# Local attention layers with the next layer's first tile computed inside the last feed-forward groups

## The chip, the cores and the metric

One Trainium2 chip, one of its cores. The metric is the time of the whole program on the device in microseconds, as the median of several runs. All data are float32, except where a table of masks and an identity are bfloat16.

## What is computed

The input is one sequence of 2048 tokens of width 128. A softmax attention block and its norm come first, then a stack of six local attention layers, then a linear attention block, then the same stack of six again, then a residual sum. The change is in the stack alone, which is run twice (its tensors have the prefixes `f_` and `g_`). Reduced to what matters, a stack is:

```python
for layer in range(6):
    h = shift_tokens(x)                       # the upper 64 features are those of the token before
    q, k, v = split(h @ Wqkv[layer], 3)       # 16 heads of 64
    q, k = l2norm(q) * q_scale, l2norm(k) * k_scale
    q, k = rotary(q, xpos_scale), rotary(k, 1 / xpos_scale)
    # token i sees keys i-32 .. i
    x = softmax(8 * q @ k.T + mask) @ v @ Wo[layer] + x
    h = layernorm(shift_tokens(x)) * g + b
    a, gate = split(h @ W1[layer] + b1, 2)    # hidden width 341
    x = (a * gelu(gate)) @ W2[layer] + b2 + x
```

## The kernel before, in words

`local_stack` (from L625) writes one instruction list by hand for each engine, as functions with the same names: `tile`, `group` and, for all, `layer`. Semaphores join them. `upto(s, L, n)` (L645) is the count that semaphore `s` has once item `n` of layer `L` is done, so an engine waits for exactly the item it needs. A loop `Fori(0, DEPTH)` runs over the six layers.

**Attention.** The 2048 tokens are 16 tiles of 128. A tile has four chunks `c`, and a step is `n = 4 t + c`, 64 steps (`STEPS`) in a layer. Chunk by chunk the projections of q half 0, k half 0, q half 1 and k half 1 are made (L1168), and in chunks 0 and 2 the values (L1185). The work of a step is spread over the following chunks, and the test `real(t, c, lag)` says whether step `n - lag` exists:

- lag 0: PE projects; ScalarE squares (L984); VectorE sums the squares (L1073); POOL raises to the power -1/2 (L928).
- lag 1: VectorE scales (L1067) and multiplies with two rope tables (L1094, L1096); POOL adds the two (L933).
- lag 2: PE transposes (L1237); ScalarE copies to `qT` or `kT` (L1013 to L1017).
- lag 4: PE makes masked scores of four heads (L1195, L1202); VectorE the maximum (L1078); ScalarE four exponentials (L1002).
- lag 5 to 7: VectorE normalises (L1084, L1087); PE transposes (L1173); ScalarE copies (L988); PE multiplies with the values (L1221); ScalarE copies to `aT` (L1024).
- In chunk 3 PE multiplies tile t-2 with `Wo` (L1231); in chunk 0 VectorE adds the residual of tile t-3 (L1063), and SP stores it to `xa` in DRAM (L843).

The values of a tile are copied to `vt` (L994), two buffers. Three transfers on SP's queue (L827 to L829) move them, with the last 32 rows of the tile before, to the windows `vw` that the value product reads. A copy to `vt` waits for the transfers of tile t-1, since these read the same buffer. For tile 1 this is the wait

```python
act.wait_ge(ld_vw[1 - q], upto(ld_vw[1 - q], L, (t - 1) >> 1, 48))
```

The tiles 0 to 2 and 13 to 15 are written out, the others are a `Fori` over pairs. After tile 15, the chunks of "tiles" 16 to 18 hold what is left of the lags.

**Feed-forward.** It has 8 groups of 256 tokens (`NF`). Stage `m` of `group` holds three groups at once: VectorE's statistics of group m+1 (L1103, L1107) and POOL's inverse deviation (L937, L939), VectorE's normalise of group m (L1119), PE's transposes (L1253) and ScalarE's Identity with gain and bias (L1033); for group m-1 PE's hidden products in three pairs (L1260, L1261), ScalarE's Gelu (L1038) and VectorE's product (L1137), giving `ag`; for group m-2 PE's output product (L1268), with POOL's bias sum (L951); and for group m-3 VectorE's output sum (L1127, `fy`) and SP's store to `xf` (L866). The hidden products have two sets of three PSUM banks.

**Between them.** Stages 0 and 1 come after the chunks of tiles 16 and 17, and stages 2 to 10 after those of tile 18. In stages 0 and 1 POOL also multiplies the rope tables with the next layer's scales (`fold_rope`, L914, L917). SP's queue is written out by hand as well: at tile 16 the next layer's `Wqkv` (L800) and the first shifted rows for the feed-forward (L852, L853), in stage 2 `Wo` (L807), in stage 6 the next layer's first two x tiles (L792, L793), in stage 9 the feed-forward weights, which are 13 transfers (L810 to L818), and in stage 10 the last store of `fy`. At the head of the layer loop PE transposes x (L1157), ScalarE copies it (L976), and the projections start.

Of the kernel before, what the change touches and what calls it, by code (L numbers as in the profile page):

```python
# [624 lines left out]
def local_stack(nc, tag, w, consts, xf, xa):  # L625
# [6 lines left out]
    with ExitStack() as ctx:  # L632
# [85 lines left out]
        STEPS = 4 * NT  # L718
        ld_ident, ld_rope, ld_mask, zeroed, act_const = (sem("ld_ident"), sem("ld_rope"), sem("ld_mask"), sem("zeroed"),
# [20 lines left out]
        dv_kzero, pl_rope = sem("dv_kzero", 1, 1), sem("pl_rope", 6)  # L740
# [13 lines left out]
        def layer(eng, body, group, L, last):  # L754


            for t in range(3):
                body(L, t, t % 2)
            with eng.Fori(0, (NT - 6) // 2) as i:
                for q in range(2):  # L760
                    body(L, 2 * i + (3 + q), (3 + q) % 2)
            for t in range(NT - 3, NT):
                body(L, t, t % 2)

            for t in range(NT, NT + 3):
                if t < last:
                    body(L, t, t % 2)
                if t < NT + 2:
                    group(L, t - NT, t % 2)
            groups(eng, group, L)  # L770

        def groups(eng, body, L):


            for m in range(2, NF + 3):
                body(L, m, m % 2)
# [19 lines left out]
        def _(sp):  # L796
# [23 lines left out]
            def tile(L, t, q):  # L820
# [12 lines left out]
                if known and t == NT:  # L833
                    sp.wait_ge(pe_qkv, upto(pe_qkv, L, STEPS - 1)).then_inc(own["sp"], 1)
                    sp.wait_ge(pl_rope, upto(pl_rope, L, 5)).then_inc(own["sp"], 1)
                    load_scales((L + 1) % DEPTH)
                    load_wqkv((L + 1) % DEPTH)
                    load_shifted(L, 0, 0)
                    load_shifted(L, 1, 1)
# [4 lines left out]
                if not known or 0 <= t - 2 < NT:  # L844
                    sp.wait_ge(st_a, upto(st_a, L, t - 4, 16)).then_inc(own["sp"], 1)
                    sp.dma_start(xr[:, q, :], rows(xf, (t - 2) * P + 1, P)).then_inc(ld_r[q], 16)

# [7 lines left out]
            def group(L, m, q):  # L855
                known = isinstance(m, int)
                if not known or m + 2 < NF:
                    load_shifted(L, m + 2, q)
                if not known or 0 <= m - 1 < NF:
# [3 lines left out]
                if not known or m >= 3:  # L863
# [5 lines left out]
                if known and m == 2:  # L869
                    sp.wait_ge(pe_Wo, upto(pe_Wo, L, NT - 1)).then_inc(own["sp"], 1)  # L870
                    load_wo((L + 1) % DEPTH)
# [18 lines left out]
            sp.wait_ge(zeroed, 5)  # L890
            with sp.Fori(0, DEPTH) as L:
                layer(sp, tile, group, L, NT + 3)

            for p in range(2):
                sp.wait_ge(ld_x[p], upto(ld_x[p], DEPTH, 0, 32))
# [7 lines left out]
        def _(pool):  # L903
# [5 lines left out]
            def fold_rope(n, kind):  # L909

                pool.wait_ge(ld_scales, upto(ld_scales, n, 0, 32))
                whole = qk_scales[:, kind, :].unsqueeze(1).broadcast_to([P, NT, DH])
                halves = qk_scales[:, kind, :].rearrange("p (a b) -> p a b", a=2)[:, ::-1, :]
                pool.tensor_tensor(rope[:, 2 * kind, :, :], rope0[:, 2 * kind, :, :], whole, ALU.mult).then_inc(pl_rope, 1)  # L914
                for a in range(2):
                    sl = slice(a * 32, a * 32 + 32)
                    pool.tensor_tensor(rope[:, 2 * kind + 1, :, sl], rope0[:, 2 * kind + 1, :, sl],  # L917
                                       halves[:, a, :].unsqueeze(1).broadcast_to([P, NT, 32]),
                                       ALU.mult).then_inc(pl_rope, 1)

            def tile(L, t, q):
                for c in range(4):
                    n, b = 4 * t + c, c % 2
                    if real(t, c, 0):

                        pool.wait_ge(dv_ssq, upto(dv_ssq, L, n)).then_inc(own["pool"], 1)
                        pool.wait_ge(dv_qh, upto(dv_qh, L, n - 2))
                        pool.tensor_tensor(rn[:, b, :], ss[:, b, :], minus_half[:], ALU.pow).then_inc(pl_rn, 1)  # L928
                    if real(t, c, 1):

                        pool.wait_ge(dv_t2, upto(dv_t2, L, n - 1))
                        pool.wait_ge(pe_qkT, upto(pe_qkT, L, n - 3))
                        pool.tensor_tensor(qr[:, 1 - b, :], t1[:, 1 - b, :], t2[:, 1 - b, :], ALU.add).then_inc(pl_qr, 1)  # L933
# [7 lines left out]
            def group(L, m, q):  # L941
                known = isinstance(m, int)
                if known and m == 0:
                    inverse_std(L, 0, 0)
                if not known or m + 1 < NF:
                    inverse_std(L, m + 1, 1 - q)
                if not known or 0 <= m - 2 < NF:
# [5 lines left out]
                if known and m < 2:  # L953
                    pool.wait_ge(dv_t2, upto(dv_t2, L, STEPS - 1))
                    fold_rope(L + 1, m)
# [3 lines left out]
            fold_rope(0, 0)  # L959
            fold_rope(0, 1)  # L960
            with pool.Fori(0, DEPTH) as L:
                layer(pool, tile, group, L, NT + 1)

        @block.scalar
        def _(act):
# [12 lines left out]
            def tile(L, t, q):  # L978
                for c in range(4):
                    n, b = 4 * t + c, c % 2  # L980
                    if real(t, c, 0):
                        act.wait_ge(pe_qkv, upto(pe_qkv, L, n))
                        act.wait_ge(dv_ssq, upto(dv_ssq, L, n - 2))
                        act.activation(sq[:, b, :], ps_qk[b][:], ACT.Square).then_inc(act_sq, 1)  # L984
                    if real(t, c, 6):
                        act.wait_ge(pe_pT, upto(pe_pT, L, n - 6))
                        act.wait_ge(pe_o, upto(pe_o, L, n - 8))
                        act.copy(pT[0:KEYS, b, :, :], ps_pT[0:KEYS, :].rearrange("p (u q) -> p u q", u=4)).then_inc(act_pT, 1)  # L988
                    if c % 2 == 0 and real(t, c, 0):
                        half = c // 2  # L990
                        act.wait_ge(pe_v, upto(pe_v, L, 2 * t + half))

                        act.wait_ge(ld_vw[1 - q], upto(ld_vw[1 - q], L, (t - 1) >> 1, 48))
                        act.copy(vt[:, q, 512 * half:512 * half + 512], ps_v[:]).then_inc(act_v, 1)  # L994
                    if c == 1 and real(t + 1, 0, 0):
# [702 lines left out]
```

## Time and profile before

| | |
|---|---|
| median of 3 runs | 5309.06 us (5306.06 to 5313.56) |
| the profiled execution | 5306.88 us |
| its span in the trace | 5304.9 us |
| stack `f`, first square to last output sum | 992 to 3025 us |
| stack `g`, first square to last output sum | 3244 to 5277 us |
| mean granted TensorE clock | 0.956 |

Two microseconds of the profiled execution lie outside the span. Each stack is some 2034 us of it, or 340 us a layer. In the rows that follow, PE is TensorE's matmul stream and PEld its weight loads, DVE is VectorE, ACT ScalarE, POOL GpSimd, and SPq the issue of transfers by SyncE. In rows of the timeline the numbers are start and duration in us; what stands in square brackets is the idle time before and what ended it ("issue" is nothing that the profile shows).

### The profile page before, as it was taken

The numbers are of one execution on the slowest core, as the hardware profiler recorded it, in microseconds if no ns is written. First come the engines' busy times: TensorE is split into PE (matmuls) and PEld (weight loads), VectorE is DVE, ScalarE is ACT, GpSimd is POOL, SyncE is SP. The second block draws the span as 40 slices with busy tenths as digits, with TensorE's granted clock in tenths as the row PEclk, the third lists the DMA queues.
The fourth block names the chain that finished last, engine by engine and source line by source line (L and its number), as shares of the span: only waits on it lengthen the run. The fifth ranks groups of instructions, "written<-read, shape, count | busy, mean of one in ns | idle before, by whom it ended". The sixth has DMA issues, their size and how long they took to land. (4 is left out here: it accounts for less than half of the span.)

```text
span 5304.9 us, 148219 instructions
## 1 busy us (share of the span) xinstructions
PE 4683.4 (88%) x45702; PEld 2936.7 (55%) x45796; DVE 4006.0 (76%) x8097; ACT 3640.1 (69%) x11776; POOL 2657.8 (50%) x2108
## 2 busy tenths in 40 slices
PE   5999999698998998989989767989989989899896
PEld 1333332366565665656666544665656656566665
DVE  7888886587786877868778546878868778687785
ACT  1777777586785876858768514867858768587684
POOL 3000000465665656656656404656656566566564
PEclk6999999899999999999999877999999999999998
DMA  0000000222222222222222302222222222222223
GB/s 13 1 2 1 2 1 1 85 58 73 57 59 77 59 71 59 59 77 59 65 66 59 85 5 85 60 75 56 57 78 60 71 61 56 77 60 69 66 54 93
DMA packets 332305, 288.20 MB, mean 54 GB/s; under 512 B 149102, under 2 KB 290964, under 8 KB 329748
## 3 DMA queue, kind: packets, MB, share of 16 engines
q1 hardware_dynamic: 331028, 281.93, 20.6%
q8 instruction: 254, 4.16, 0.3%
q14 instruction: 255, 2.09, 0.1%
q10 hardware_dynamic: 768, 0.02, 0.0%
HBM read 100.42 MB, written 30.41 MB: 25 GB/s over the span
## 5 line engine op out<-in xcount | busy, mean ns | idle before, releaser
L928 POOL TENSOR_TENSOR f_rn<-f_ss,f_minus_half 128x8 f32<-128x8 f32 x384 | 636.9, 1658 | 302.0 <-DVE f_ss L1073 297.1
L928 POOL TENSOR_TENSOR g_rn<-g_ss,g_minus_half 128x8 f32<-128x8 f32 x384 | 636.8, 1658 | 301.2 <-DVE g_ss L1073 296.3
L425 DVE TENSOR_REDUCE a_maxima<-a_max 128x1 f32<-128x512 f32 x1024 | 651.8, 687 | 147.4 <-PE a_max L539 110.4
L1002 ACT ACTIVATE f_ex<-f_bank,f_nmx 128x96 f32<-128x96 f32 x1536 | 502.9, 339 | 226.3 <-DVE f_nmx L1078 226.3
L1002 ACT ACTIVATE g_ex<-g_bank,g_nmx 128x96 f32<-128x96 f32 x1536 | 502.9, 339 | 226.2 <-DVE g_nmx L1078 226.2
L349 ACT ACTIVATE a_pex<-a_scores 128x512 f32<-128x512 f32 x1024 | 531.6, 606 | 159.3 <-PE a_scores L548 158.5
L933 POOL TENSOR_TENSOR g_qr<-g_t 128x512 f32<-128x512 f32 x384 | 488.4, 1272 | 269.6 <-DVE g_t L1096 269.6
L933 POOL TENSOR_TENSOR f_qr<-f_t 128x512 f32<-128x512 f32 x384 | 488.4, 1272 | 268.7 <-DVE f_t L1096 268.7
L1168 PE MATMUL g_bank<-g_wqkv,g_xT 128*128 128x512 f32 x768 | 407.9, 614 | 29.9 <-ACT g_xT L976 24.1
L1168 PE MATMUL f_bank<-f_wqkv,f_xT 128*128 128x512 f32 x768 | 407.0, 612 | 29.9 <-ACT f_xT L976 24.5
L1073 DVE TENSOR_REDUCE f_ss<-f_sq 128x8 f32<-128x512 f32 x384 | 263.5, 686 | 209.7 <-ACT f_sq L984 195.4
L1073 DVE TENSOR_REDUCE g_ss<-g_sq 128x8 f32<-128x512 f32 x384 | 263.5, 686 | 209.0 <-ACT g_sq L984 195.6
L539 PE MATMUL a_max<-a_stackT 128*128 128x512 bf16 x963 | 345.8, 396 | 22.1 <-DVE a_maxima L425 14.0
L280 POOL COPY a_v_head<-a_v_all 128x128 f32 (+1 forms) x16 | 4.6, 290 | 694.2 <-PE a_sums L557 694.2
L548 PE MATMUL a_scores<-a_stackT 128*128 128x512 bf16 x991 | 308.6, 382 | 27.3 <-ACT a_pex L349 20.2
L1002 ACT ACTIVATION_READ_ACCUMULATOR f_ex<-f_bank,f_nmx 128x1 f32 x1536 | 311.4, 203 | 0.0
L1002 ACT ACTIVATION_READ_ACCUMULATOR g_ex<-g_bank,g_nmx 128x1 f32 x1536 | 311.3, 203 | 0.0
L1237 PE MATMUL f_bank<-f_ident,f_qr 128*128 128x128 f32 x1536 | 248.3, 284 | 47.9 <-POOL f_qr L933 47.3
L1237 PE MATMUL g_bank<-g_ident,g_qr 128*128 128x128 f32 x1536 | 248.7, 285 | 47.5 <-POOL g_qr L933 46.3
L1173 PEld LDWEIGHTS f_bank<-f_ident,f_pn 128*96 128x96 f32 x1536 | 173.3, 126 | 206.7 <-DVE f_pn L1087 123.2
L1173 PEld LDWEIGHTS g_bank<-g_ident,g_pn 128*96 128x96 f32 x1536 | 172.9, 126 | 207.0 <-DVE g_pn L1087 122.9
L1067 DVE SCALAR_TENSOR_TENSOR f_qh<-f_rn,f_bank 128x512 f32<-128x512 f32 x384 | 261.5, 681 | 28.8 <-POOL f_rn L928 28.8
(238 smaller groups left out, 12000.6 us busy)
## 6 DMA issues: line engine op xcount, KB each, us to landing
f_vw<-f_vt SPq DMA_DIRECT2D x96, 384.0 KB, 4.2
g_vw<-g_vt SPq DMA_DIRECT2D x96, 384.0 KB, 4.3
f_vw<-f_vt SPq DMA_DIRECT2D x96, 256.0 KB, 3.6
g_vw<-g_vt SPq DMA_DIRECT2D x96, 256.0 KB, 3.6
f_vw<-f_vt SPq DMA_DIRECT2D x96, 128.0 KB, 2.3
g_vw<-g_vt SPq DMA_DIRECT2D x96, 128.0 KB, 2.3
f_wqkv<-in_f_Wqkv_dram SPq DMA_DIRECT2D x7, 1536.0 KB, 9.5
g_wqkv<-in_f_Wqkv_dram SPq DMA_DIRECT2D x7, 1536.0 KB, 9.3
```

The lines of the kernel that those rows point to most:

```text
L349: act.activation(pex[:, kt % 2, i % NG, :], ps_s[i % 3][:], ACT.Exp).then_inc(act_ex, 1)
L425: dve.tensor_reduce(maxima[:, m // 4, m % 4:m % 4 + 1], ps_max[m % 3][:], AX.X, ALU.max).then_inc(dv_max, 1)
L539: pe.matmul(ps_max[m % 3][:], stackT[:, slot, 0, P * (m // 4):P * (m // 4) + P], stackT[:, slot, 1, GQ * (m % 4):GQ * (m % 4) + GQ], start ...
L548: pe.matmul(ps_s[i % 3][:], stackT[:, slot, 1, P * kt:P * kt + P], stackT[:, slot, 0, GQ * g:GQ * g + GQ], start=True, stop=True).then_inc ...
L928: pool.tensor_tensor(rn[:, b, :], ss[:, b, :], minus_half[:], ALU.pow).then_inc(pl_rn, 1)
L933: pool.tensor_tensor(qr[:, 1 - b, :], t1[:, 1 - b, :], t2[:, 1 - b, :], ALU.add).then_inc(pl_qr, 1)
L1002: last = act.activation(ex[:, b, u, :], ps_s[:, h, KEYS * jj:KEYS * jj + KEYS], ACT.Exp, bias=nmx[:, b, u:u + 1], accum_out=sm[:, b, u:u + 1])
L1067: dve.scalar_tensor_tensor(out=heads(qh[:, 1 - b, :]), in0=rn[:, 1 - b, :].unsqueeze(2).broadcast_to([P, 8, DH]), scalar=1e12, in1=heads(p ...
L1073: dve.tensor_reduce(ss[:, b, :], heads(sq[:, b, :]), AX.X, ALU.add).then_inc(dv_ssq, 1)
L1168: pe.matmul(ps_qk[b][:], xT[:, q, :], wqkv[:, at:at + 512], start=True, stop=True).then_inc(pe_qkv, 1)
L1173: last = pe.transpose(ps_pT[0:KEYS, P * u:P * u + P], pn[:, b, u, :], ident[:])
L1237: last = pe.transpose(ps_qkT[:, P * j:P * j + P], qr[:, b, P * j:P * j + P], ident[:])
```

## The change

The loop over layers is rotated. `tile` becomes `chunk`, one call for one chunk, and `group` becomes `stage`. The four chunks of tile 0 of the next layer run inside stages 6 to 9 of this layer; the first layer's are run by `head` ahead of the loop. In the last layer of the stack they are computed as well, and nothing reads them. The left-over chunks 64 to 72 are dealt out over stages -2 to 2.

- The statistics start two stages ahead and the normalise one stage ahead. On PE the first hidden pair comes before the transposes, and on ScalarE the first Gelu before the Identity; on VectorE the output sum comes first and the three products are spread between the others.
- PSUM banks are dealt out anew (`ps_f`, `ps_h`, `freed`). From group 2 on the hidden products have one set of banks, 6, 7 and 4.
- The rope tables are folded in four slices of four tiles, in stages 1 to 4, both kinds in each.
- On SP's queue the first shifted rows are loaded at tile 15 and `Wqkv` last in tile 16; the next x tiles and `Wo` in stage 4; and the feed-forward weights in stage 10, after the last store of `fy`. The v windows of tile 0 are issued by tile 1's chunk 0, after the jump to the loop's head.

Its core (the bodies that are only moved one level out are left out):

```diff
-        ps_h = [[banks[0], banks[7], banks[3]], [banks[4], banks[6], banks[2]]]
-        ps_fT = banks[1]
-        ps_f = banks[5]
+        ps_f = [banks[0 if m < 3 else 5] for m in range(NF)]
+        ps_h = [[banks[i] for i in ((1, 3, 6), (7, 1, 3))[m]] if m < 2 else [banks[6], banks[7], banks[4]] for m in range(NF)]
+        freed = [-6, -6, -6, -6, 0, 1, 2, 3, -6]
...
+            seam = [(-2, 1), (-1, 1), (0, 2), (1, 2), (2, 3)]
+            n = STEPS
+            for m, chunks in seam:
+                stage(L, m)
+                for k in range(n, n + chunks):
+                    chunk(L, k // 4, k // 4 % 2, k % 4)
+                n += chunks
+            for m in range(3, 6):
+                stage(L, m)
+            for m in range(6, 10):
+                stage(L, m)
+                chunk(L + 1, 0, 0, m - 6)
+            stage(L, NF + 2)
...
         # SP, stage
-                if known and m == NF - 2:
+                if m == 4:
                     for p in range(2):
                         sp.wait_ge(pe_xT, upto(pe_xT, L, NT - 2 + p)).then_inc(own["sp"], 1)
                         load_xs(sp, L + 1, p, p)
-                if known and m == NF + 1:
+                    sp.wait_ge(pe_Wo, upto(pe_Wo, L, NT - 1)).then_inc(own["sp"], 1)
+                    load_wo((L + 1) % DEPTH)
+                if m == NF + 2:
                     sp.wait_ge(pe_out, upto(pe_out, L, NF - 1)).then_inc(own["sp"], 1)
                     sp.wait_ge(pl_b2, upto(pl_b2, L, NF - 1)).then_inc(own["sp"], 1)
                     load_wf((L + 1) % DEPTH)
...
         # POOL, stage
+                if 0 <= m - 1 < NR:
                     pool.wait_ge(dv_t2, upto(dv_t2, L, STEPS - 1))
-                    fold_rope(L + 1, m)
+                    fold_rope(L + 1, NT // NR * (m - 1), NT // NR, 1)
+                if m + 2 < NF:
+                    inverse_std(L, m + 2, q)
...
         # ACT, stage
+                if 0 <= m - 1 < NF:
+                    gelu(L, m - 1, 0)
+                if 0 <= m < NF:
...
+                    act.activation(xnT[:, m % 2, :], ps_f[m][:, 0:FQ], ACT.Identity, bias=ln_b[:], scale=ln_g[:]).then_inc(act_fT, 1)
+                if 0 <= m - 1 < NF:
+                    gelu(L, m - 1, 1)
+                    gelu(L, m - 1, 2)
...
         # DVE, stage: output sum (m - 3), product 0 (m - 1), normalise (m + 1), product 1 (m - 1),
         # statistics (m + 2), product 2 (m - 1); at m == 2 also the memset of kT's first columns
...
         # PE, stage
+                if 0 <= m - 1 < NF:
+                    pe.wait_ge(act_fT, upto(act_fT, L, m - 1))
+                    hidden(L, m - 1, 0)
+                if 0 <= m < NF:
...
+                        last = pe.transpose(ps_f[m][:, P * s:P * s + P], xn[:, m % 2, s, :], ident[:])
...
+                if 0 <= m - 1 < NF:
+                    hidden(L, m - 1, 1)
+                    if m == 1:
+                        pe.wait_ge(act_exp, upto(act_exp, L, STEPS - 1))
+                    hidden(L, m - 1, 2)
+                if 0 <= m - 2 < NF:
+                    # the output product of group m - 2 waits for its products, for sum m - 3
+                    # and for the Identity of group m
...
         # PE, chunk
+                if known and n == 0:
+                    pe.wait_ge(dv_y, upto(dv_y, L - 1, NT - 1)).then_inc(own["pe"], 1)
+                    transpose_x(L, 0, 0)
+                    pe.wait_ge(ld_wqkv, upto(ld_wqkv, L, 0, 16))
```

## Rows read from the trace of the kernel before

**Rows 1.** The page, busy time and share of the span by engine.
```profile
PE 4683.4 (88%) x45702; PEld 2936.7 (55%) x45796; DVE 4006.0 (76%) x8097; ACT 3640.1 (69%) x11776; POOL 2657.8 (50%) x2108
```
**Rows 2.** Stretches: length, busy PE, PEld, DVE, ACT, POOL, granted clock; steady attention, drain.
```profile
1564.00:1598.00 34.00, 33.37 (x395) 22.57 (x393) 29.40 (x59) 28.62 (x106) 23.37 (x16) 1.00 0.22 56
1598.00:1617.00 19.00, 14.94 (x230) 11.63 (x228) 11.43 (x29) 13.79 (x58) 6.39 (x6) 1.00 0.48 144
```
**Rows 3.** Timeline, layer 1: last square, last scores, output of tile 14, first statistics.
```profile
1598.33 0.64 ACT L984 ACTIVATE f_sq<-f_bank 128x512 f32<-128x512 f32 x1
...
1612.88 0.56 PE L1202 MATMUL f_bank<-f_kT,f_qT 64*64 64x96 f32 x16
...
1613.99 2.05 PE L1231 MATMUL f_bank<-f_wo,f_aT 128*128 128x128 f32 x16
...
1614.66 0.48 DVE L1103 BATCH_NORM_STATS2 f_st<-f_fxs 128x6 f32<-128x128 f32 x2
...
1615.29 0.25 DVE L1107 BATCH_NORM_AGGREGATE f_mv<-f_st 128x2 f32<-128x6 f32 x2 [0.15 <-DVE f_st L1103]
...
1616.79 0.60 DVE L1119 TENSOR_SCALAR f_xn<-f_fxs,f_mv,f_rstd 128x128 f32<-128x128 f32 x2 [1.25 <-POOL f_rstd L939]
```
**Rows 4.** Timeline, layer 1's feed-forward: slow and full pairs, transposes of groups 3 and 6.
```profile
1631.06 1.02 PE L1261 MATMUL f_bank<-f_xnT,f_w 128*128 128x256 f32 x2
...
1636.65 0.44 PE L1253 MATMUL f_bank<-f_ident,f_xn 128*128 128x128 f32 x2 [0.25 <-DVE f_xn L1119]
...
1637.36 0.59 PE L1261 MATMUL f_bank<-f_xnT,f_w 128*128 128x256 f32 x2
...
1650.51 0.44 PE L1253 MATMUL f_bank<-f_ident,f_xn 128*128 128x128 f32 x2 [0.25 <-DVE f_xn L1119]
```
**Rows 5.** Timeline, end of layer 1 and start of layer 2.
```profile
1665.83 0.42 DVE L1127 TENSOR_TENSOR f_fy<-f_bank,f_fx 128x256 f32<-128x256 f32 x1 [1.85 <-DMA xf<-f_fy]
1666.02 0.37 SPq L810 DMA_DIRECT2D f_w<-in_f_W_dram  x1
...
1668.48 0.35 PE L1157 MATMUL f_bank<-f_ident,f_xs 128*128 128x128 f32 x1 [2.77 <-issue]
...
1674.52 0.40 SPq L866 DMA_DIRECT2D xf<-f_fy  x1
...
1686.53 0.59 ACT L994 COPY f_vt<-f_bank 128x512 f32<-128x512 f32 x1 [0.33 <-PE f_bank L1185]
...
1689.75 0.63 ACT L984 ACTIVATE f_sq<-f_bank 128x512 f32<-128x512 f32 x1
```
**Rows 6.** Timeline, the seam before: layer 0's last square, layer 1's value copy and square.
```profile
1256.99 0.64 ACT L984 ACTIVATE f_sq<-f_bank 128x512 f32<-128x512 f32 x1
...
1348.04 0.59 ACT L994 COPY f_vt<-f_bank 128x512 f32<-128x512 f32 x1 [1.17 <-PE f_bank L1185]
...
1350.99 0.63 ACT L984 ACTIVATE f_sq<-f_bank 128x512 f32<-128x512 f32 x1
```
**Rows 7.** Busy time in stretches as in rows 2, after the jump between layers 0 and 1.
```profile
1327.30:1334.10 6.80, 4.58 (x6) 2.03 (x7) 0.69 (x1) 2.36 (x4) 0.44 (x1) 0.50 0.22 41
```
**Rows 8.** Timeline, POOL: the bias sum over 256 columns, and a rope fold over 1024.
```profile
1638.91 0.72 POOL L951 TENSOR_TENSOR f_fx<-f_fx,f_b 128x256 f32<-128x256 f32 x1
...
1619.68 2.35 POOL L914 TENSOR_TENSOR f_rope<-f_rope,f_qk_scales 128x1024 f32<-128x1024 f32 x1
```
**Rows 9.** The page's transfers: the largest of the three v windows, median to landing.
```profile
f_vw<-f_vt SPq DMA_DIRECT2D x96, 384.0 KB, 4.2
```
**Rows 10.** Timeline, end of stack f: first of the 13 weight loads, last store.
```profile
3025.24 0.37 SPq L810 DMA_DIRECT2D f_w<-in_f_W_dram  x1
...
3031.80 0.40 SPq L866 DMA_DIRECT2D xf<-f_fy  x1
```
**Rows 11.** Instructions of lines L976 and L1038: the table loads among them.
```profile
L976 ACT ACT_TABLE_LOAD  x12: 1283/1283/1283, 988.5 to 4939.4; - x12
L1038 ACT ACT_TABLE_LOAD  x12: 1283/1283/1283, 1284.2 to 5236.7; - x12
```

More of the change, by code:

```diff
@@ L890, in _ @@
             sp.wait_ge(zeroed, 5)
+            head(chunk)
             with sp.Fori(0, DEPTH) as L:
-                layer(sp, tile, group, L, NT + 3)
+                layer(sp, chunk, stage, L)
             for p in range(2):
-                sp.wait_ge(ld_x[p], upto(ld_x[p], DEPTH, 0, 32))
+                sp.wait_ge(ld_x[p], upto(ld_x[p], DEPTH, 1 - p, 32))
             sp.wait_ge(ld_wqkv, 16 * (DEPTH + 1))
@@ L907, in _, with fold_rope @@
             pool.memset(kT[:], 0.0).then_inc(zeroed, 1)
-            def fold_rope(n, kind):
+            def fold_rope(n, first, count, each):
                 pool.wait_ge(ld_scales, upto(ld_scales, n, 0, 32))
[L912 to L933, printed above, removed]
+                ts = slice(first, first + count)
@@ L939, in inverse_std, with stage @@
                 pool.tensor_tensor(rstd[:, q, :], var[:, q, :], minus_half[:, 0:FT], ALU.pow).then_inc(pl_rstd, 1)
[L941 to L947, printed above, removed]
+            def stage(L, m):
+                q = m % 2
+                if 0 <= m - 2 < NF:
                     pool.wait_ge(ld_wf, upto(ld_wf, L, 0, 13 * 16))
@@ L1044, in _ @@
             put_mask()
+            head(chunk)
             with act.Fori(0, DEPTH) as L:
-                put_xT(L, 0, 0)
-                act.wait_ge(dv_kzero, upto(dv_kzero, L, -1))
-                layer(act, tile, group, L, NT + 2)
+                layer(act, chunk, stage, L)
         @block.vector
@@ L1140, in _ @@
+                if m + 2 < NF:
+                    row_stats(L, m + 2, m % 2)
+                if 0 <= m - 1 < NF:
+                    product(L, m - 1, 2)
+                if m == 2:
+                    dve.wait_ge(pe_s, upto(pe_s, L, STEPS - 1))
+                    dve.memset(kT[:, :, P:P + WINDOW], 0.0).then_inc(dv_kzero, 1)
             for buf in (vt, vw, pT):
                 dve.memset(buf[:], 0.0).then_inc(zeroed, 1)
+            head(chunk)
             with dve.Fori(0, DEPTH) as L:
[L1143 removed]
@@ L1144, in _ @@
-                layer(dve, tile, group, L, NT + 3)
-                dve.wait_ge(pe_s, upto(pe_s, L, STEPS - 1))
-                dve.memset(kT[:, :, P:P + WINDOW], 0.0).then_inc(dv_kzero, 1)
+                dve.wait_ge(pl_rope, upto(pl_rope, L, 6 * NR - 1)).then_inc(own["dve"], 1)
+                layer(dve, chunk, stage, L)
         @block.tensor
@@ L1275, in _ @@
             pe.wait_ge(ld_ident, 16)
+            head(chunk)
             with pe.Fori(0, DEPTH) as L:
-                transpose_x(L, 0, 0)
-                pe.wait_ge(ld_wqkv, upto(ld_wqkv, L, 0, 16))
                 pe.wait_ge(ld_wo, upto(ld_wo, L, 0, 16)).then_inc(own["pe"], 1)
-                layer(pe, tile, group, L, NT + 2)
+                layer(pe, chunk, stage, L)
 def linear_attention(nc, tag, x_in, w, consts, x_out, xf):
```

488 lines of the change are left out of this document (250 added, 238 removed).

## The prediction

> **What bounds the kernel now.** I read the page first: TensorE is busy 88% of the span and VectorE 76% [rows 1], so on average nothing has much to give. That average hides the place of this change. Both local stacks are six layers long, and a layer is a long stretch of attention followed by a feed-forward. The stage table shows the steady attention with PE busy 33.37 of 34.00 us, and the first 19 us of the drain with 14.94 [rows 2]. The change touches only this end, the feed-forward and the next start. So I measure every event from one mark, the start of the layer's last square of a projection on ScalarE, at 1598.33 [rows 3].
>
> From that mark, in this layer: the last scores are computed at +14.6 [rows 3]; group 3 of the feed-forward is transposed at +38.3, group 6 at +52.2 [rows 4]; the last output sum ends at +67.9; PE then idles 2.77 us on "issue", at the jump back to the loop's head; the second 128 tokens' first value copy (f_vt, L994) starts at +88.2, the next square (of step 5) at +91.4 [rows 5]. The seam before took 91.1 and 94.0 [rows 6]: after the jump the granted clock was 0.50 for 6.8 us [rows 7], the lower of the two levels, and in that seam again later. I take the means of the two, +89.6 and +92.7. These are the marks to beat. The stretch is a chain of hand-offs (projection, square, sum, power on POOL, scaling, rope, transposes), not a full engine.
>
> **The change, part by part.** Ten seams between layers have the whole change; the last layer of each stack has all its costs and no next layer.
>
> Drain and groups 0 to 2. Statistics and normalising (0.48 + 0.15 + 0.25 and 0.60) go between the last chunks. The first statistics fit in VectorE's idle time; the next ones and the first normalise come before the maximum of step 61 and push it by 0.75. The Identity copy (0.57) on ScalarE falls in the same chain, so the last scores start at +15.2 and not +14.6, and the last exponentials end at +17.8 [rows 3]. PE does the output sum of tile 14 (2.05) and then group 0's first hidden pair, ended at +19.4. Table load (1.28), three Gelus (0.47 each) and the Identity bring ScalarE to +22.5; VectorE's three products, a normalise, statistics and the delayed probabilities end at +24.8. PE's last probability transpose and value product go to +26.0, group 1's hidden pairs and a transpose (2.6 + 0.3) to +28.9, group 0's output (1.42) to +30.3, the last value product, its copy and the output of tile 15 to +33.5, one hidden pair (0.86), and group 3 is transposed at +34.4 where it was +38.3. In the old order the granted clock fell here once; a pair at the low level takes 1.02 to 1.06 where it takes 0.59 [rows 4]. I add 1.0 for the same fall (bounds 0 and 1.4): +35.4, so **2.9 won**.
>
> Groups 3 to 5. The old period is 4.62 ((52.2 - 38.3) / 3): the transposes wait 0.25 for a normalise that stands behind the last product [rows 4]. In the new order a hidden pair covers that wait. PE's own work is 0.27 + 3 x 0.86 + 1.42 = 4.28. One set of hidden banks where there were two costs nothing: a bank is free as soon as its product is made, 1.6 us after its pair starts, and is wanted 4.28 later. The rope fold is the same work in four slices; POOL needs about 0.7 for 256 columns [rows 8], so a slice is about 3.2, and with a bias sum (0.73) and the inverse deviation (about 1.0) a stage is 5.0. It begins a stage early and has slack from the seam. Statistics of group 5 wait for SP, held until tile 15's row store: 0.3. Three stages are 13.1: group 6 at +48.5, **3.7 won** so far.
>
> Groups 6, 7 and the end, with four chunks of the next layer. The old stretch from here to the last sum is 15.7. New, along PE: rest of stage 6 3.4; x transpose, copy, first projection and values 2.5; stage 7 4.6, of which 0.3 waits for the output sum, which is behind a square sum on VectorE; chunk 1 1.15; stage 8 4.4, 0.4 of it such a wait; chunk 2 2.2; stage 9 3.2, 1.8 of it such a wait (behind two rope products); then projection 3, square, square sum, two rope products and the last output sum, 1.02 + 0.65 + 0.7 + 1.25 + 0.42 = 4.0. Sum 25.4: the last sum ends at +73.9, **6.0 later** than before, but with four steps done that used to take 13.7 us from first to fifth square.
>
> The wait that replaces the start-up. From here the engines could go on at once: the fifth square would come about 2 us later, near +76, and the value copy at +77.3. But the copy overwrites a buffer that the three v-window copies read, and ScalarE waits for these transfers. SP issues them after the jump, and in the new order the 13 loads of the next feed-forward weights stand in front. Before, they started when the last output product ended, 0.2 before the last sum was done, and lay beside the start-up [rows 5]. Now SP waits for the last output sum, stores it, waits as before for PE and POOL, issues 13 loads, and only then the v windows. Chain: 0.2 to SP, 0.5 for the store, 8.5 for the loads to the next issue [rows 5], 0.3 for the loop's end, 1.2 until the third window's issue, 4.2 to its landing [rows 9]: 14.9. Bounds: 6.6 for the loads as at a stack's end [rows 10] gives 13.0; a landing a microsecond later behind the weights gives 15.9. The copy starts at +88.8, against +89.6. Queued behind it on ScalarE are all the exponentials, so PE stands idle some 11 us. On release the exponentials need not wait for the maximum, which has long been there, so the next square is 2.4 behind the copy, not 3.1: 0.7 won. The idle time surely costs clock: an idle of 2.77 was followed by 6.8 us at 0.50 [rows 5, 7]. During the restart this costs between 0 and 3.4; I take 0.9, since hand-offs fill most of it.
>
> One seam: -0.8 - 0.7 + 0.9 = -0.6 us; ten: **-6**.
>
> Ends of the stacks. The last layer computes four useless chunks, so its last sum is 6.0 later. Before, the last store was issued 6.6 after the first weight load [rows 10], so 6.3 after the sum, whose end is 0.2 behind that load's issue [rows 5]; it landed about 2 later. Now the store goes first, but the block ends with the weight loads, some 9.2 after the sum, 0.8 more. Twice 6.8: **+13.6**. The start of each stack has the same steps in the same order: nothing.
>
> Sum +7.6 on the profiled execution's own 5306.9 is 5314.5. That execution lies 2.2 below the median 5309.1, so 5316.7, rounded down to **5316 us**. About 0.2%, 10.6 us, is what a measurement of this kernel can tell from no change; the forecast lies within it, near its edge.
>
> **The rivals.**
> *A, the wait does not bite*: the start-up is simply hidden. For it: the engines would be at the copy by +77.3. A seam then gains 12.3, so 5309 - 123 + 14 = 5200. Against it: SP issues in order, and the loads' time is in the trace. Chance 0.06.
> *B, the merged stretch runs better*: no fall of the clock in the drain (1.0) or during the release (0.9), no late statistics (0.3), and 6.6 us of loads (1.9). Each seam gains 4.1 more: 5275. For it: bounds of mine, each seen once. Against: all must hold. 0.17.
> *C, slower: VectorE's order sets the merged stages.* The output sum stands behind the chunk's square sum and rope products, and PE's transposes or output stand behind that sum. My waits of 0.3, 0.4 and 1.8 are differences of long sums. If each of the four pairs takes 1 us more, the last sum, SP's loads and the copy all shift by 4: 10 x 4 + 2 x 4 is 48 at most, less where the low clock hides in a wait; 5355. It decides from 0.6 us a seam upwards, where nothing is won any more. Chance 0.22.
> *D, table loads.* There are two per layer, 1.28 each, one at the first Gelu and one at the loop's head [rows 11]; squares and exponentials share one set, and no row shows a square under Gelu's. If it needs the other set, a seam has four more loads, two at squares and two at Gelus, about 5 us, all ahead of the last sum: 5316 + 12 x 4.5 = 5370. Chance 0.05. The Trainium skill (ScalarE: Activation LUTs, Table sets: the hidden batching unit) speaks against the interleaving: activations are to be batched by set. The same section says that cheap functions such as copy and identity stand in every set, without naming the square there, and its section What ACT_TABLE_LOAD costs puts a switch at 2.66 us with the drain; by that figure the four would cost about 10.6 us a seam. The trace has 1.28 for the load itself and an Identity and Gelus side by side with no further load.
>
> **How the numbers follow.** The forecast as worked has 0.50, with its own range 5296 to 5336; of this 0.05 is faster by over 0.2%, 0.29 within, 0.16 slower. A and B are faster, C and D slower. Faster 0.05 + 0.06 + 0.17 = 0.28, within 0.29, slower 0.16 + 0.22 + 0.05 = 0.43. The range 5276 to 5356 takes in B and C and leaves out A, D and the tails.
>
> **What would show it.** In the changed kernel: group 3 transposed about +35 and a period of 4.3 for groups 3 to 5; the last output sum near +74; ScalarE idle some 11 us before the value copy of every layer's tile 1 but the first, ended by the f_vw transfer; the 13 weight loads between the last store and the v windows on SP's queue; low clock in that gap; two table loads a layer. The prediction is wrong if that copy waits for nothing (A), if the last sum comes before +71 (B) or after +76 (C), or if squares have table loads before them (D).

## The result, and the profile after

The changed kernel takes 5428.5 us (median of 4 runs, 5423.2 to 5430.0), the kernel before on the same chip 5307.6: ratio 1.023, 95% interval 1.0217 to 1.0242. That is 121 us slower. The forecast was 5316 with a range to 5356, so it was **wrong** in the size. "Slower" had the largest of its three chances, 0.43, but the point that it gave lay within 0.2% of the kernel before. The profiled execution has a span of 5420.7 us against 5304.9.

The page, busy time by engine. These lines answer to [rows 1]:
```profile
PE 4725.8 (87%) x45840; PEld 2958.5 (55%) x45840; DVE 3989.7 (74%) x8123; ACT 3639.7 (67%) x11798; POOL 2706.7 (50%) x2338
```
No engine does much more work. PE is busy for 42 us more, with 138 more instructions and a lower mean clock (0.941, before 0.956). The rest of the 116 us is idle time of PE, and the question is what it waits for.

I measured both kernels as the prediction does, from the start of a layer's last square (here 1605.40), and took the mean over the ten seams. The column "forecast" repeats the prediction's marks. Differences in the text are taken before rounding.

| start at, us after the mark | before | forecast | after | after, stack f | after, stack g |
|---|---|---|---|---|---|
| last scores | 14.5 | 15.2 | 19.6 | 19.2 | 19.9 |
| group 3 transposed | 38.3 | 35.4 | 40.1 | 39.9 | 40.4 |
| group 6 transposed | 52.2 | 48.5 | 55.2 | 54.8 | 55.5 |
| end of the last output sum | 68.0 | 73.9 | 80.5 | 80.0 | 81.1 |
| first weight load issued | 67.7 | about 74.6 | 81.6 | 80.9 | 82.3 |
| first v window issued | 81.5 | - | 91.9 | 88.9 | 94.8 |
| value copy of tile 1 | 89.6 | 88.8 | 97.5 | 94.6 | 100.4 |
| square of step 5 | 92.7 | 91.2 | 99.7 | 96.8 | 102.6 |

Three losses are to be read from it. In both stacks the last scores are over 4 us later than forecast. Groups 3 to 5 take 15.0 us instead of 13.1. And stack g loses another 4.5 us between the first weight load and the first v window (12.5 us against 8.0 in f). The stretch with the four chunks of the next layer, from group 6 to the last output sum, takes 25.4 us, as forecast.

Timeline, the drain of layer 1: SyncE's queue first, then VectorE and ScalarE, then PE. What stands in brackets is the idle time before the row and what ended it:
```profile
1612.99 0.33 SPq L809 DMA_DIRECT2D f_wqkv<-in_f_Wqkv_dram  x1
1614.92 0.39 SPq L864 DMA_DIRECT2D f_fxs<-xa  x1
1615.36 0.75 SPq L865 DMA_DIRECT2D f_fxs<-xa  x1
...
1616.73 0.60 DVE L1154 TENSOR_SCALAR f_xn<-f_fxs,f_mv,f_rstd 128x128 f32<-128x128 f32 x2
...
1621.24 0.48 DVE L1121 BATCH_NORM_STATS2 f_st<-f_fxs 128x6 f32<-128x128 f32 x2 [3.90 <-DMA f_fxs<-xa]
...
1622.09 0.56 DVE L1096 TENSOR_REDUCE f_nmx<-f_bank 128x4 f32<-128x384 f32 x1
...
1622.68 0.34 ACT L1015 ACTIVATE f_ex<-f_bank,f_nmx 128x96 f32<-128x96 f32 x1 [3.32 <-DVE f_nmx L1096]
...
1624.72 0.92 PE L1231 MATMUL f_bank<-f_kT,f_qT 64*64 64x96 f32 x16
1626.62 2.75 PE L1260 MATMUL f_bank<-f_wo,f_aT 128*128 128x128 f32 x16
```
The rows of group 2 (f_fxs) are issued 1.9 us behind the next layer's Wqkv. VectorE's statistics of group 2 want them at 1617.34 and get them at 1621.24. The maximum of step 62 is behind these statistics in VectorE's order, ScalarE's exponentials wait for it, and the last scores (1624.72, +19.3) wait for those. The page's transfers show the size of what is ahead:
```profile
f_wqkv<-in_f_Wqkv_dram SPq DMA_DIRECT2D x7, 1536.0 KB, 7.9
f_fxs<-xa SPq DMA_DIRECT2D x96, 64.0 KB, 3.1
```
1612.99 + 7.9 is 1620.9, just before the statistics start. In the kernel before, this load was issued at 1600.14, 1.8 us behind the mark and not 7.6, and nobody waited for the rows behind it: the statistics came behind the attention and, at 1614.66, had no wait [rows 3].

The same drain as a stretch (columns as in rows 2); it answers to the second line there:
```profile
1605.40:1624.60 19.20, 13.14 (x182) 9.86 (x174) 13.02 (x36) 11.85 (x49) 9.45 (x13) 0.82 0.48 144
```
The granted clock is 0.82 where it was 1.00: the scores take 0.92 and the output product 2.75, where they took 0.56 and 2.05 [rows 3]. All twelve drains of this kernel have 6.8 or 10.2 us at the lower level, starting 12 to 15 us behind the mark. Before, there was one fall of 3.4 us, near +32.

Groups 3 to 5, SyncE's queue in stage 4 and VectorE in stage 5:
```profile
1651.03 0.40 SPq L801 DMA_DIRECT2D f_xs<-xf  x1
...
1653.13 0.39 SPq L816 DMA_DIRECT2D f_wo<-in_f_Wo_dram  x1
1653.91 0.37 SPq L864 DMA_DIRECT2D f_fxs<-xa  x1
1654.41 0.38 SPq L865 DMA_DIRECT2D f_fxs<-xa  x1
...
1657.99 0.48 DVE L1121 BATCH_NORM_STATS2 f_st<-f_fxs 128x6 f32<-128x128 f32 x2 [1.47 <-DMA f_fxs<-xa]
```
Four loads of x and one of Wo (2.9 us of SyncE) stand ahead of the rows of group 7, which are wanted at 1656.52.

The end of the layer, where the forecast stall is. Last output sum; SyncE's first and last weight loads and first v window; ScalarE:
```profile
1684.90 0.41 DVE L1142 TENSOR_TENSOR f_fy<-f_bank,f_fx 128x256 f32<-128x256 f32 x1
...
1686.20 1.39 SPq L819 DMA_DIRECT2D f_w<-in_f_W_dram  x1
...
1693.28 0.38 SPq L827 DMA_DIRECT2D f_b<-in_f_b_dram  x1
1694.33 0.56 SPq L838 DMA_DIRECT2D f_vw<-f_vt  x1
...
1686.07 1.28 ACT L997 ACT_TABLE_LOAD   x1 [2.21 <-issue]
1687.45 0.60 ACT L997 ACTIVATE f_sq<-f_bank 128x512 f32<-128x512 f32 x1
1699.81 0.58 ACT L1007 COPY f_vt<-f_bank 128x512 f32<-128x512 f32 x1 [11.76 <-DMA f_vw<-f_vt]
```
This is the wait that the prediction named, at its length ("some 11 us"): 14.5 us from the end of the sum to the copy, 14.9 forecast. In stack g the same wait is 15.4 to 16.8 us.

Groups of instructions by line. Before the bar the busy time and the mean ns, behind it the idle time before the group and what ended it. These are the two waits over all layers:
```profile
L1007 ACT COPY g_vt<-g_bank 128x512 f32<-128x512 f32 x194 | 116.2, 599 | 98.9 <-DMA g_vw<-g_vt 80.1 <-PE g_bank L1214 17.7
L1007 ACT COPY f_vt<-f_bank 128x512 f32<-128x512 f32 x194 | 116.2, 599 | 75.1 <-DMA f_vw<-f_vt 57.1 <-PE f_bank L1214 17.1
L1121 DVE BATCH_NORM_STATS2 g_st<-g_fxs 128x6 f32<-128x128 f32 x96 | 23.0, 281 | 42.9 <-DMA g_fxs<-xa 42.9
L1121 DVE BATCH_NORM_STATS2 f_st<-f_fxs 128x6 f32<-128x128 f32 x96 | 23.0, 281 | 35.7 <-DMA f_fxs<-xa 35.7
```

### The profile page after: what moved, and what is told of

It is laid out like the page before. It is cut to its first block and busy times, and to the rows that moved or that the text cites. A ratio compares the mean times of both kernels' runs of the same rounds, so it can differ in the third digit from the quotient of the medians.

```text
span 5420.7 us, 148975 instructions
## 1 busy us (share of the span) xinstructions
PE 4725.8 (87%) x45840; PEld 2958.5 (55%) x45840; DVE 3989.7 (74%) x8123; ACT 3639.7 (67%) x11798; POOL 2706.7 (50%) x2338
## 5 line engine op out<-in xcount | busy, mean ns | idle before, releaser
L539 PE MATMUL a_max<-a_stackT 128*128 128x512 bf16 x1024 | 369.5, 398 | 12.5 <-issue 6.8
L997 ACT ACTIVATE f_sq<-f_bank 128x512 f32<-128x512 f32 x388 | 241.9, 623 | 60.5 <-PE f_bank L1197 58.2
L997 ACT ACTIVATE g_sq<-g_bank 128x512 f32<-128x512 f32 x388 | 241.9, 623 | 60.1 <-PE g_bank L1197 57.7
L1250 PE MATMUL g_bank<-g_pT,g_vw 128*64 128x64 f32 x6144 | 268.0, 231 | 7.9
```

The lines of the kernel that those rows point to most:

```text
L539: pe.matmul(ps_max[m % 3][:], stackT[:, slot, 0, P * (m // 4):P * (m // 4) + P], stackT[:, slot, 1, GQ * (m % 4):GQ * (m % 4) + GQ], start ...
L1250: last = pe.matmul(ps_o[r, at:at + BLK], vw[:, p, blk, P * j + DH * h:P * j + DH * h + DH], pT[:, 1 - b, 2 * h + jj, BLK * blk:BLK * blk + ...
```

## The experiments

All nine runs that follow are of the changed kernel with the edit named. Two theories went in: **W**, the v windows come late, and **D**, rows for VectorE's statistics come late and hold the attention's last steps. Against them: the merged stages' order (the prediction's rival C), the clock, and the loop's jump. Chips and hours shift both kernels a little, so I compare each run by its distance to the kernel before, measured beside it (the changed kernel: +121). Where an expectation says "the fifth square", it means the square of step 5; only the one "4.3 us behind the last fy" in run 5 is tile 1's first square.

**1. Windows first.** In SyncE's program:
```
 stage 9:        + three copies vw <- vt of tile 0
 chunk of t=1:   - three copies vw <- vt of tile 0
```


> Edit: the three copies that make tile 0's V windows are issued in stage 9, right after the last chunk of tile 0, so ahead of the last fy store, of the 13 weight loads and of the loop's jump, instead of behind all three. Theory W (the windows are late, and ScalarE's second value copy of tile 1 waits for them): the wait of 11.8 us in front of that copy goes, the next limit is the first square of tile 1, which stands 2.7 us behind the last fy. The fifth square behind the last square of the layer before then starts at about +87 instead of +96.7 in stack f and +102.4 in stack g: -10 us in each of five seams of f, -15 in each of g, 5428 - 125 = about 5300 us. Rival J (the jump to the loop's head, 2.9 us on PE, 2.2 on ScalarE and 5.2 on SyncE in stack g, is what is waited for; windows are only the last of it): SyncE is still late in g, PE and ScalarE wait as long for other things, g gains no more than f, 5428 - 70 to 90 = 5340 to 5360. Rival C (the merged stages' order costs everywhere): under 30 us gained.

Measured: 5326.9 us, ratio 1.004 (1.0025 to 1.0054), +23. So 98 of the 121 are gone, less than the 125 expected and far more than rival C allowed. At the square of step 5, stack g gains 10.9 us a seam and f 5.3; rival J allowed g no more than f. The copy of tile 1's values starts 5.9 us behind the last sum (87.8 and 81.9), not 17.0. In the seam of layer 1:
```profile
1683.12 1.28 ACT L1002 ACT_TABLE_LOAD   x1 [3.75 <-issue]
1685.06 0.60 ACT L1002 ACTIVATE f_sq<-f_bank 128x512 f32<-128x512 f32 x1 [0.65 <-PE f_bank L1202]
1686.85 0.59 ACT L1012 COPY f_vt<-f_bank 128x512 f32<-128x512 f32 x1 [1.19 <-PE f_bank L1219]
...
1682.95 2.07 PE L1202 MATMUL f_bank<-f_wqkv,f_xT 128*128 128x512 f32 x2 [4.59 <-issue]
```
The stall is gone, and the jump is next: PE idles 4.59 us there (2.87 with the stall behind it) and ScalarE 3.75 (2.21). In six of the ten seams the clock falls a second time near +30, and the mean distance from group 1's transpose to group 3's grows from 15.3 to 16.9 us. These two are some 1.6 us a seam each. That is of the size of the missing 27, and no closer than that: the profiled execution is 12 us slower than the median.

**2. Wqkv in pieces.**
```
 chunk of t=NT:  - load_wqkv(next layer)            (1.5 MB)
 stages 0 to 5:  + load_wqkv(next layer, piece m)   (256 KB, behind the shifted rows of group m+2)
```


> Edit: the next layer's 1.5 MB of Wqkv is loaded in six pieces of 256 KB, one behind each of the loads of the shifted rows of groups 2 to 7, instead of in one transfer ahead of the rows of group 2. Theory D (VectorE's statistics of group 2 wait 3.9 us for rows that lie behind the 7.9 us of the large load, and the maximum of step 62 stands behind them): that wait shrinks to under 1 us, the layer's last scores come at +15.5 to +16.5 instead of +19.6, group 3's first transpose at +36.5 instead of +40.1, and ten seams of 3.5 us give about 5393 us. Rival K (TensorE's lower clock in the drain, or VectorE's longer order of work, sets it): last scores stay within 1 us of +19.6, time within 10 us of 5428. Rival P (the pieces take the place of the one load and each delays the rows of its stage): last scores earlier by 3.5 us but group 6 as late as before at +55.2, no gain in sum.

Measured: 5364.9 us, 1.0111 (1.0094 to 1.0128), +61. Last scores at +16.8 instead of +19.6, group 3 at +37.2, group 6 at +52.4: theory D holds and most of the gain is carried on, so rivals K and P fall as the main cause. In stack f 1.8 of 2.9 us are left at the square of step 5, where the clock falls near +53 in three of its five seams. In layer 1 the wait is down from 3.90 us to:
```profile
1617.64 0.49 DVE L1123 BATCH_NORM_STATS2 f_st<-f_fxs 128x6 f32<-128x128 f32 x2 [1.08 <-DMA f_fxs<-xa]
```
In stack g it is 0.2 us or less. The low clock in the drains shrinks to 3.4 or 6.8 us, but it does not go away with the wait: five of stack g's six drains still have a fall. The 60 won are more than the 35 expected, because stack g's 4.5 us between weight loads and windows are gone too (7.8 us in f, 8.1 in g). Nothing in the edit touches that place. Run 9 asks why.

**3. x and Wo one stage later**, behind the rows of group 7.
```
 - if m == 4:  load_xs(next layer, tiles 0 and 1), load_wo(next layer)
 + if m == 5:  the same
```


> Edit: the loads of the next layer's first two x tiles and of Wo are issued in stage 5 behind the shifted rows of group 7 instead of in stage 4 ahead of them. Theory Q (the five issues in stage 4 hold SyncE's queue, so the rows of group 7 come late and the statistics of group 7 wait 1.5 us): stage 5 takes about 4.4 instead of 5.9 us, group 6's first transpose comes at +53.7 instead of +55.2, ten seams give 15 us: about 5413. Rival (stage 5 is long for another reason, such as the order of the Gelus and the products): no change, 5428.

Measured: 5402.1 us, 1.0181 (1.0164 to 1.0198), +98. Groups 3 to 5 take 13.0 us, where the forecast had 13.1 and the changed kernel 15.0: theory Q holds. Group 6 comes at +54.2, not +53.7, since a second fall of the clock near +30, as in run 1, puts group 3 at +41.2. Of the 23 us won, 7 lie in the linear attention block, ahead of stack g's first square, which this edit should not touch; run 9 finds the same 7 us there.

**4. Weights behind the windows**, both in tile 1's first chunk, behind the jump.
```
 stage 10:       - load_wf(next layer)
 chunk of t=1:   three copies vw <- vt of tile 0
                 + wait for the last layer's last fy, load_wf(this layer)
```


> Edit: the 13 loads of the feed-forward weights are issued in tile 1's first chunk, behind the copies of tile 0's V windows, instead of ahead of them; the copies stay behind the last fy store and behind the loop's jump. If the 13 issues are the whole price in both stacks (12.5 us between first weight load and first window copy in g, 8.1 in f), the copies are issued 7.5 us earlier in f and 12 in g: 5428 - 98 = 5330, less up to 7 us at each stack's end. If in g some 5 us of it belong to the jump of SyncE to the loop's head, g gains only 7.5 as f does: 5428 - 75 = 5353, less the ends. The first experiment's theory puts this kernel 4 to 9 us a seam behind that one, since 0.5 us of issue, the jump and 4.2 us of copy remain between the last fy and the value copy.

Measured: 5328.1 us, 1.0049 (1.0032 to 1.0066), +24. The windows are issued 1.2 us behind the last sum in f and 4.0 us in g; 3 us of the difference between the stacks are still there with no weight load near. In the seam of g (last fy store, first window):
```profile
3931.39 0.37 SPq L881 DMA_DIRECT2D xf<-g_fy  x1
3935.35 0.57 SPq L838 DMA_DIRECT2D g_vw<-g_vt  x1
```
So most of g's extra time is at SyncE's jump to the loop's head. From one layer's mark to the next, g gains 9.4 us and f 6.8; for g this is between the two cases expected. The last part of the expectation failed: this kernel is level with run 1 (+24 and +23), and not 4 to 9 us a seam behind it. From the last sum to the square of step 5 it takes 9.7 us in f and 12.1 in g, run 1 10.1 and 9.3, and its stacks' ends are shorter, since no weights are loaded there.

**5. Four moves together**: windows in stage 9, weights in tile 1's first chunk, pieces, x in stage 5.


> Edit: four moves in SyncE's order together: tile 0's windows in stage 9, the 13 weight loads in tile 1's first chunk behind the loop's jump, Wqkv in six pieces, x and Wo in stage 5. If the waits are separate and add up: windows first 5327, less 1.8 us a seam because PE and ScalarE jump to the loop's head with fewer transfers beside them (the fifth square came 4.3 us behind the last fy with the weights beside the jump, 2.5 with them behind it), less 3.5 a seam for the pieces, less 1 to 1.5 for x: 5327 - 18 - 35 - 12 = about 5262 us, below the kernel before (5304). Rival (one wait only takes the place of the next, the merged stages being the floor): the gains overlap and it stays at 5300 to 5327.

Measured: 5223.7 us, ratio **0.9844** (0.9831 to 0.9858), 88 us faster than the kernel before and 209 less than the change as it was, by the distances. The waits were separate and their gains add: runs 1 to 3 alone had won 98, 60 and 23. The two waits over all layers, against the rows of the changed kernel:
```profile
L1012 ACT COPY g_vt<-g_bank 128x512 f32<-128x512 f32 x194 | 116.3, 600 | 21.8 <-PE g_bank L1219 20.7
L1012 ACT COPY f_vt<-f_bank 128x512 f32<-128x512 f32 x194 | 116.3, 600 | 22.1 <-PE f_bank L1219 21.1
L1126 DVE BATCH_NORM_STATS2 f_st<-f_fxs 128x6 f32<-128x128 f32 x96 | 23.0, 281 | 9.4 <-DMA f_fxs<-xa 9.3
L1126 DVE BATCH_NORM_STATS2 g_st<-g_fxs 128x6 f32<-128x128 f32 x96 | 23.0, 281 | 3.4 <-DMA g_fxs<-xa 3.1
```
The statistics' wait is 12 us in all instead of 79, the value copies' wait for windows is gone from 137. It is 38 us better than expected: the stacks' ends (83.1 and 82.3 us from the last square to the next block, 94.3 and 95.4 in the changed kernel, 81.9 and 82.2 before) were not in my sum. One part of the expectation failed: with the weights behind the jump it was to be 2.5 us from the last sum to tile 1's first square, and it stays at 4.1:
```profile
1333.34 0.41 DVE L1147 TENSOR_TENSOR f_fy<-f_bank,f_fx 128x256 f32<-128x256 f32 x1
...
1335.62 2.07 PE L1202 MATMUL f_bank<-f_wqkv,f_xT 128*128 128x512 f32 x2 [4.33 <-issue]
```

**6. No rotation**, everything else as changed: tile 0's chunks at the head of their own layer.
```
 for t in range(1, 3)              ->  for t in range(0, 3)
 stages 6 to 9: chunk(L + 1, 0, 0, m - 6), and head(chunk)   ->  gone
```


> Edit: the rotation alone is undone: tile 0's four chunks run at the head of their own layer again, behind stage 10; the new drain, the smaller stages, the banks and SyncE's drain loads stay as in the changed kernel. Theory W+D (the drain and groups 3 to 5 lost 3 us a seam, the rotation lost by late windows and the ends of the stacks): group 6's first transpose stays at +55, the last fy comes 15.8 us behind it as in the kernel before instead of 25.3, the value copy 37.4 us behind it (+92.6, against +94.6 in f and +100.4 in g), and no unused tile at each stack's end: 5428 - 10 - 39 - 13 to 24 = about 5360 us. Rival R (the rotation is what costs, everywhere): under 5330. Rival S (rotation gains, the drain loses all): 5428 or more.

Measured: 5347.9 us, 1.0066 (1.0051 to 1.0082), +36. The last sum ends 14.4 us behind group 6's transpose, the value copy starts 36.0 behind it (37.4 expected), in f and g alike. As changed, the rotation costs 85 us, 68 were expected; neither rival fits. One part of the expectation failed: group 6 comes at +56.9 and not at +55, since the second fall of the clock near +30 appears in five of the ten seams.

**7. No rotation, drain mended**: run 6 with Wqkv in pieces and x in stage 5.


> Edit: as the run without rotation, and Wqkv in six pieces and x and Wo in stage 5 as in the four moves. It prices the rotation itself once nothing else is late. If the rotation is worth what its chain says: group 6 comes at +50 as with the four moves (5224 us), the fifth square 40.5 us behind it, as in the kernel before, instead of 34.0, so 6.5 us a seam more, the stacks' ends about as long: 5224 + 65 = about 5290 us. Rival (the gain of the four moves is all in the drain and the rotation gives nothing): within 15 us of 5224.

Measured: 5310.1 us, 0.9997 (0.9988 to 1.0006) of the kernel before. Against run 5 it is 86 us slower: the same rotation that costs 85 us with late windows is worth 86 without them (65 expected). From group 6's transpose to the square of step 5 it is 40.2 us here and 34.0 there. Group 6 itself is 1.6 later, since the second fall of the clock appears in four of stack f's five seams here and in none there. So some 16 of the 86 us are that fall, and not the rotation's chain.

**8. Statistics of group 2 behind step 62**, added to run 5, in VectorE's program:
```
 stage 0:                 - row_stats(L, 2, 0)
 end of chunk STEPS + 2:  + row_stats(L, 2, 0)
```


> Edit: as the four moves together, and VectorE's statistics of group 2 stand behind the attention's step 62 work instead of ahead of its maximum. Theory D says that with the pieces about 1.1 us of wait and 0.9 us of statistics still stand in the chain of scores: last scores 1.5 to 2 us earlier, 1 to 2 us a seam, 10 to 20 us less than the four moves alone. Rival: group 2's normalise comes as much later and takes it back: no change.

Measured: 5225.0 us, 0.984 (0.9826 to 0.9853): no difference to run 5. The last scores come 0.4 us earlier (+16.4), not 1.5 to 2, and group 3 at +36.7 in both. So what was left of the wait was hardly in the chain of scores. What group 3 does follow is the clock. These are two drains of run 5, layers 1 and 2, from the mark to group 3's transpose (columns as in rows 2):
```profile
1590.20:1625.60 35.40, 28.09 (x347) 22.58 (x341) 21.05 (x63) 20.83 (x73) 20.44 (x34) 1.00 0.26 68
1920.01:1957.10 37.09, 30.42 (x347) 24.35 (x340) 21.05 (x63) 20.95 (x73) 20.38 (x34) 0.91 0.25 65
```
The statistics of group 2 wait 0.85 us in the first and 1.01 in the second. The first has the full clock throughout, the second 6.8 us of low clock. Runs 2, 5 and 8 have 36 drains. Four of them have no fall of the clock ahead of group 3, and it comes at +35.3; in eleven with one fall of 3.4 us near +15 it comes at +36.4 to +36.8; in seventeen with one of 6.8 us near +12 at +36.9 to +37.4. The other four have a fall near +26 to +29.

**9. Eight repeated waits on SyncE**, ahead of the weight loads.
```
 + for _ in range(8): sp.wait_ge(pe_out, upto(pe_out, L, NF - 1))
```


> Edit: the changed kernel with eight repeats of a wait that is already over ahead of the weight loads on SyncE, nothing else; it moves the code behind it. In the changed kernel first weight load to first window copy takes 8.1 us in stack f and 12.5 in stack g; with the pieces of Wqkv it took 8.2 in both. Theory L (the 4.4 us more are the jump of SyncE to the loop's head, and hang on where the code lies): the time in f or g changes by 4 to 5 us a seam with this edit, either way, the kernel by about 20 us. Rival (they belong to stack g's loads or to what else is in the queues there): both stay, 5428 within 8.

Measured: 5399.8 us, 1.0167 (1.0151 to 1.0182), +88: **33 us faster** than the changed kernel, with eight instructions more and nothing else. SyncE's queue in stack g, last weight load and first window, in the changed kernel:
```profile
4699.60 0.38 SPq L827 DMA_DIRECT2D g_b<-in_f_b_dram  x1
4705.22 0.58 SPq L838 DMA_DIRECT2D g_vw<-g_vt  x1
```
The same two rows of this kernel:
```profile
3989.05 0.38 SPq L827 DMA_DIRECT2D g_b<-in_f_b_dram  x1
3990.09 0.55 SPq L838 DMA_DIRECT2D g_vw<-g_vt  x1
```
5.6 us and 1.0 us for the same step. Stack f is as it was (80.9 to 88.8). Of the span's 27 us, 19 are in g's five seams and 7 in the linear attention block between the stacks. Theory L holds: the step to the loop's head changes with nothing but SyncE's code. Run 2, which changes that code as well, also has 1.0 us there in stack g. That the place of the code decides is the reading that is left; why one place is slow no row shows.

## Why the prediction was wrong

**The wait at the end was right.** Windows late by the 13 loads, 14.9 us forecast and 14.6 measured in f (19.3 in g, see the third step); low clock behind it; about 11 us of idle ScalarE. Run 1 shows that it is causal. Rival A priced its absence at 116 us less; taking it away gave 98.

**The merged stages were right.** "Sum 25.4": measured 25.4. Rival C did not happen, although its test fired: the last sum does come "after +76" (+80.5), but the lateness was all there at group 6. A test of an absolute mark can't tell where the time was lost; the difference of two marks can.

**The step that failed is the drain.** The prediction wrote "the last scores start at +15.2" and "+35.4, so 2.9 won". It costed the statistics as 0.48 + 0.15 + 0.25 of VectorE and never asked when their rows arrive. It put Wqkv's load, which the change issues right in front of group 2's rows, at no cost. That was true in the old order, where the statistics came behind the attention, and it is false once they stand in the chain of scores. The trace of the kernel before shows how long such rows take. There too four loads of rows were issued behind Wqkv, between 1599 and 1604 (time to landing at the end):
```profile
f_wqkv<-in_f_Wqkv_dram SPq DMA_DIRECT2D x1, 1536.0 KB, 9.4
f_fxs<-xa SPq DMA_DIRECT2D x4, 64.0 KB, 7.1
```
The rows took 7.1 us, and nobody waited for them. The change put a waiting engine behind them. The measured +40.1 is 4.7 us later than forecast, and run 2 took back 2.9 of it. What remains is 1.8, and the rows are not its cause: in run 2 stack g waits for them 0.2 us or less and has its last scores at +16.6 all the same. It goes with the clock (the count is under run 8). Without a fall group 3 comes at +35.3, where the prediction has 34.4; it adds 1.0 for a fall, and one costs 1.1 to 2.1.

**The second is the same oversight, smaller.** "Statistics of group 5 wait for SP ...: 0.3. Three stages are 13.1": they were 15.0, because it is group 7's rows that wait, behind x and Wo. Without these the stages take 13.0 (run 3). PE's period of 4.28 was near (4.35 in run 3); a DMA queue was the bound that PE's sum had left out.

**The third could not be read from before.** "0.3 for the loop's end" on SyncE: from the last weight load to the first window, the load's own 0.4 included, it is about 1 us in f and 5.6 in g. With the 13 loads, f took 8.0 where 8.8 was forecast, and g 12.5. Where it was short in g as well, the span was 27 us shorter and the time 33 (run 9). In the kernel before, the jump lay beside the start-up.

**The sum.** The forecast's own is +7.6. Drain and stages, (4.7 + 1.9) x 12 layers, are 79, since the stacks' ends have both delays too (they grew by 12.4 and 13.2 us, 6.8 was forecast). Run 9's 27 come on top, of which 19 are g's seams and 7 the linear attention block. Together this is 114, of 115.8 in the spans. Another 3.4 us come ahead of stack f's first mark, where "nothing" was forecast and no term stands. So the total closes only because a few us cancel by luck.

**Rival D** (table loads) fell: 12 on either line, as before. Squares ran between Gelus and behind the last of them, at +60, +66, +72 and +77, with none in front. The Trainium skill (ScalarE: Activation LUTs, Table sets: the hidden batching unit) has the rule to batch activations by set; interleaving them cost nothing here, because the square brought no table load.

Still open: why it takes 4.1 to 4.3 us and not 2.6 from the last sum to tile 1's first square when the windows were copied before it (runs 1 and 5). Code moved in both runs, so run 9's cause and the traffic of the windows can't be told apart. Open too is what sets off the second fall of the clock near +30; it comes and goes with edits that are nowhere near it.

## What to carry to other kernels

When work is moved into a chain, list its inputs' arrival as carefully as its instructions: for each DMA that feeds it, find what is issued in front and how many bytes that is. Read the time to landing of such a load in the old trace even where nobody waited for it. A load that was free where it stood is not free when a waiting engine's order changes; cut it into pieces and put each behind the small loads that somebody waits for. The same rearrangement went with 86 us less or 85 us more, depending on the order of one DMA queue, so try a losing change again with its queue mended before undoing it.

## What the hardware showed that was not expected

A 64 KB load takes 3.1 us at the median. Two that were issued 1.9 and 2.4 us behind 1.5 MB took 5.1 and 5.9 us: the first landed 0.8 us before the large one, the second 0.4 us after it. The Trainium skill (DMA: Bandwidth & Descriptors, Queues, rings and completion order) says that each DMA engine takes descriptors in the order of its ring, though completion is not first in, first out for the queue as a whole. The trace agrees with both halves: the small loads are held up by the large one, and one of them still lands ahead of it.

Eight instructions that do nothing made the kernel 33 us faster: SyncE's step to the loop's head in stack g took 5.6 us in one kernel and 1.0 in the other, for the same source. 7 us more were won in a block that the edit does not touch. An effect under 0.6% in a kernel with loops may be of this kind; a second edit of equal length and no meaning tells.

A wait of about 4 us in the drain went with 6.8 to 10.2 us at 1.2 GHz instead of 2.4 in the changed kernel, and the clock came back by itself. In run 5 it was 3.4 or 6.8 us, and none in two of the ten seams. But in stack g of that run VectorE waits 0.2 us or less for the rows, and all six drains have 6.8 us. And in run 7 four of stack f's drains have 10.2 us with a wait of 0.4 to 0.6 us. So the length of the wait does not set the length of the fall. What does is open; the kernel before has no fall at this place.
